# Clamped cross attention: the limits moved from the scores to the probabilities

## The chip, the cores and the metric

One core of a Trainium2 chip runs the whole program in one launch. The metric is the device time of that launch in microseconds; lower is better.

## The reference

A perceiver with 32 sequences of 32 tokens of 256 channels and a context of 257 rows of 192 channels for each sequence. Fourteen stages follow one another, among them four cross attentions. Two of these, of level 0 and level 1, are computed by the function that is changed. What they compute:

```
q = layernorm(x) @ Wq + bq        # 16 heads of 16
k = ctx @ Wk + bk;  v = ctx @ Wv + bv
s = scale * q @ k.T
s = clip(s, -10000, 10000)        # level 1 only
p = softmax(s)                    # over 257 context rows
x = x + (p @ v) @ Wo + bo
```

## The kernel before

`cross_attention` (L738) handles one sequence after another; the text calls one a batch, n = 0 to 31, and four of them a group (128 tokens). The engines' programs are written out by hand as queues that meet in semaphores. The order of each queue is fixed, and an instruction that waits holds all behind it.

For batch n, TensorE (`keys_values`) makes the keys and values of batch n + 1 from the context, turns the probabilities of batch n (`turn_probs`, L833: two pairs of score rows, four transposes each, each pair behind its own `probs_ready`) and then makes the scores of batch n + 1 (`scores`, L816). In the second and third batch of a group two of four parts of the products with values of the previous group stand between these (`probs_values`, L847, L853), in the fourth the turning of its outputs and the output product.

ScalarE (`exponentials`, L937) computes exp(score + nmax) for four rows of 257 columns in two pairs; between the pairs it evicts the keys of the next batch (`take_keys`, L927). Behind them comes its copy of the turned probabilities (L957).

VectorE (`maxima`, L1065) reduces each pair of score rows to the negated maximum `nmax`. With a clamp, L1062 first writes the clamped scores to the tile `sc` in SBUF, and both the reduction and the exponential read `sc`; without one both read PSUM. Its queue in a batch is: normalise the outputs (fourth batch of a group only, L1075 and L1077), evict the values (L1053), add to x (first batch only, L1082), round the context of batch n + 3 (L1048), copy the turned probabilities (L1108), mask the tails (first batch, L1069), statistics (third batch, L1086), maxima of n + 1.

GpSimd splits the context behind VectorE's rounding (L987, L990), spreads the queries (L979) and keeps the 257th column of the probabilities (L996) once both pairs are ready. SyncE loads the context three batches ahead.

The level 0 stage runs from about 22 to 213 us of the span, the level 1 stage, with `clamp=1.0e4`, from about 568 to 773 us. Only the latter has L1062.

Of the kernel before, what the change touches and what calls it, by code (L numbers as in the profile page):

```python
# [18 lines left out]
ALU = mybir.AluOpType  # L19
ACT = mybir.ActivationFunctionType  # L20
# [3 lines left out]
P = 128  # L24
# [713 lines left out]
def cross_attention(k, w, qt, given, clamp=None):  # L738

    nc = k.nc  # L740
# [4 lines left out]
             "tails_ready values_placed turned_done turned_act turned_dve tails_turned tail_masked pv_done rsum_ready o_ready ot_done "  # L745
             "ot_ready y_done y_added noted")
    with stage(k, names) as (block, s), \
            buffers(k, t0=[P, B], t1=[DK - P, B], vtail=[B, 16, 17], key=[P, 2, DC, LK], val=[P, 2 * BT, 2, 16, 17], qx=[P, 2, DC, 2, S],
                    p=[P, 2, 4, LK], nmax=[P, 2, 4], pt=[P, 2 * BT, 2, 4, DC, 2, S], tails=[P, 2, P], tail_values=[P, 2, 16, 17],
                    own_tails=[P, BT, DC, 2, S], rsum=[P, 16], o=[P, 16, 16], ot=[P, DC, P],  # L750
                    sc=[P, 4 if clamp else 1, LK if clamp else 1]) as b, \
            buffers(k, F32R, w=[P, 2, 2, 2 * D], c=[P, 3, 2, LP], clo=[P, 3, LP]) as r:
# [170 lines left out]
        def _(act):  # L923
# [6 lines left out]
            def exponentials(n, par, first):  # L930
                if not first:
                    act.wait_ge(s.tails_ready, n - 1)
                for r4 in range(4):
                    if r4 % 2 == 0:
                        act.wait_ge(s.max_ready, 2 * n + 1 + r4 // 2)
                    score = b.sc[:, r4, :] if clamp else k.ps[:, SB + r4, 0:LK]
                    last = nc.scalar.activation(b.p[:, par, r4, :], score, ACT.Exp, bias=b.nmax[:, par, r4:r4 + 1])  # L937
                    if r4 % 2:
                        last.then_inc(s.probs_ready, 1)
                    if r4 == 1 and n + 1 < B:  # L940
                        take_keys(n + 1, 1 - par)
# [19 lines left out]

            act.wait_ge(*w.at)
            for u, part in ((0, w.wk), (1, w.wv)):
                nc.scalar.copy(r.w[:, 0, :, u * D:(u + 1) * D], part).then_inc(s.w_hi, 1)
# [10 lines left out]
        def _(pool):  # L975
# [26 lines left out]
            def body(it, first, last):  # L1002
                for gpar in range(2):
                    group = 2 * it + gpar
                    for j in range(BT):
# [12 lines left out]
                        if not (last and gpar == 1 and j == BT - 1):  # L1018
                            keep_tails(n + 1, (j + 1) % 2, gpar if j < BT - 1 else 1 - gpar, (j + 1) % BT)

            for t, ordered in ((given.t0, b.t0), (given.t1, b.t1)):
                nc.gpsimd.tensor_copy(ordered[:].rearrange("p (b t) -> p b t", b=BT),
                                      t[:].rearrange("p (t b) -> p b t", b=BT)).then_inc(s.t_ordered, 1)
                pool.wait_ge(s.t_ordered, 1 if ordered is b.t0 else 2)
# [18 lines left out]
        def _(dve):  # L1043
# [12 lines left out]
            def maxima(n, par):  # L1056
                dve.wait_ge(s.scores_done, n + 1)
                for half in range(2):
                    rs = slice(2 * half, 2 * half + 2)
                    score = k.ps[:, SB + rs.start:SB + rs.stop, 0:LK]  # L1060
                    if clamp:
                        nc.vector.tensor_scalar(b.sc[:, rs, :], score, clamp, -clamp, ALU.min, ALU.max).then_inc(s.clamped, 1)  # L1062
                        dve.wait_ge(s.clamped, 2 * n + 1 + half)
                        score = b.sc[:, rs, :]
                    nc.vector.tensor_reduce(b.nmax[:, par, rs], score, AX.X, ALU.max, negate=True).then_inc(s.max_ready, 1)  # L1065

# [25 lines left out]
            def body(it, first, last):  # L1092
                for gpar in range(2):
                    group = 2 * it + gpar
                    begin, end = first and gpar == 0, last and gpar == 1
                    for j in range(BT):
                        n = group * BT + j
                        final = end and j == BT - 1
                        if j == 3 and not begin:
                            normalize_outputs(group - 1)  # L1100
                        if not final:
                            take_values(n + 1, gpar * BT + j + 1 if j < BT - 1 else (1 - gpar) * BT)
# [2056 lines left out]
```

## Time and profile before

| | |
|---|---|
| median of 3 runs | 1841.16 us (1838.53 to 1845.12) |
| the profiled execution | 1834.88 us |
| its span, first to last instruction | 1833.0 us |
| PE matmul busy | 1553.4 us (85%) |
| DVE busy | 964.6 us (53%) |
| ACT busy | 748.2 us (41%) |
| POOL busy | 534.4 us (29%) |
| mean granted clock of TensorE | 0.928 of full speed |

Shares of the whole span are averages over fourteen stages with different limits, so this table does not say what an edit to one stage is worth. PE is TensorE's matmul, DVE is VectorE, ACT is ScalarE, POOL is GpSimd. Durations of matmuls overlap, since they are pipelined, and neighbouring instructions of an engine overlap at their ends too; the distance between two starts is then shorter than the duration of the first.

### The profile page before, as it was taken

Reading aid. Unit: us, or ns where it says so; the run is one execution under the profiler, and the core shown is the slowest. Engines: PE = TensorE matmul, PEld = TensorE weight load, DVE = VectorE, ACT = ScalarE, POOL = GpSimd, SP = SyncE. Lnnn points to the kernel's source line nnn. Section 1 sums busy time; section 2 is a strip of 40 time slices with the busy share of each in tenths; the row PEclk is TensorE's granted clock in tenths of the full one; section 3 lists DMA queues with packets and bytes.
Section 4 is the critical chain, followed back from the end, with each engine's and each line's share of the span. In section 5 each row is a group of like instructions: output and inputs, shape, how many; then the busy total and the mean of one; then the engine's idle time right before and its main releaser. Section 6 shows DMA issues by size and latency. Waiting matters only on the chain. (4 is left out here: it accounts for less than half of the span.)

```text
span 1833.0 us, 44725 instructions
## 1 busy us (share of the span) xinstructions
PE 1553.4 (85%) x17451; PEld 1311.3 (72%) x17451; DVE 964.6 (53%) x2131; ACT 748.2 (41%) x1714; POOL 534.4 (29%) x699
## 2 busy tenths in 40 slices
PE   6999745799996999795999879997787998888894
PEld 5888644599975777674888768984675985666784
DVE  5666468611117888657222257664655773466323
ACT  3555455333433555351233236663133423445122
POOL 3444235032213443160444222220011210433341
PEclk9999877899998999897999989999887999898897
DMA  4211010198862111021899743330101119311696
GB/s 146 53 51 44 6 41 11 58 352 321 330 225 80 49 49 49 7 50 72 283 319 313 265 150 102 91 92 11 45 2 39 46 52 289 84 33 43 208 314 206
DMA packets 103107, 228.36 MB, mean 125 GB/s; under 512 B 36184, under 2 KB 56152, under 8 KB 95776
## 3 DMA queue, kind: packets, MB, share of 16 engines
q1 hardware_dynamic: 91008, 200.06, 33.8%
q0 software_dynamic: 8160, 22.29, 3.2%
q10 hardware_dynamic: 3776, 3.67, 0.6%
q8 instruction: 122, 2.00, 0.4%
q14 instruction: 41, 0.34, 0.1%
HBM read 206.12 MB, written 19.79 MB: 123 GB/s over the span
## 5 line engine op out<-in xcount | busy, mean ns | idle before, releaser
L2434 PEld LDWEIGHTS ps<-xt,w 128*128 128x128 f32 x1728 | 202.3, 192 | 37.8 <-issue 26.2
L2434 PE MATMUL ps<-xt,w 128*128 128x128 f32 x1728 | 211.2, 278 | 18.4 <-DMA w<-in_L_ffn_w 14.4
L2487 ACT ACTIVATE g<-ps,b 128x128 f32<-128x128 f32 x340 | 124.3, 367 | 245.1 <-PE ps L2434 220.5
L2444 PE MATMUL ps<-w,g 128*128 128x256 f32 x864 | 200.7, 379 | 0.3 <-ACT g L2487 0.3
L2444 PEld LDWEIGHTS ps<-w,g 128*128 128x128 f32 x864 | 157.5, 190 | 18.5 <-ACT g L2487 0.6
L2528 POOL DMA_INDIRECT results<-y,dest x85 | 83.8, 986 | 253.8 <-DVE y L2656 253.8
L2648 DVE COPY xt<-ps 128x256 f32<-128x256 f32 x85 | 36.1, 424 | 195.4 <-PE ps L2424 195.4
L2523 POOL DMA_INDIRECT x<-rows,token x85 | 82.7, 973 | 166.8 <-DVEq L2623 141.8
L2656 DVE COPY y<-ps 128x256 f32<-128x256 f32 x85 | 36.1, 425 | 161.9 <-PE ps L2444 161.9
L797 PE MATMUL ps<-c,w 128*128 128x258 f32 x512 | 93.4, 294 | 7.7 <-DVE pt L1108 6.4
L937 ACT ACTIVATE p<-sc,nmax 128x257 f32<-128x257 f32 x128 | 58.1, 503 | 81.3 <-DVE nmax L1065 81.3
L441 PE MATMUL ps<-consts_sb,z_sb 128*128 128x128 f32 x176 | 39.6, 416 | 59.2 <-DVE z_sb L627 59.2
L807 PE MATMUL ps<-w,c 128*128 128x256 f32 x512 | 89.2, 287 | 0.1
L797 PEld LDWEIGHTS ps<-c,w 128*128 128x128 f32 x512 | 74.7, 189 | 19.9 <-issue 17.7
L1053 DVE TENSOR_TENSOR val<-ps,store_sb 128x512 f32<-128x512 f32 x64 | 44.2, 690 | 82.3 <-PE ps L807 82.1
L2129 PE MATMUL ps<-x,w 128*128 128x512 f32 x288 | 78.8, 414 | 7.7 <-DVE w L2292 7.7
L459 PE MATMUL ps<-x,w 128*128 128x512 f32 x336 | 81.1, 399 | 3.5 <-DVE x L639 2.4
L604 POOL TENSOR_TENSOR w<-store_sb,w 128x512 fp32r<-128x512 f32 (+1 forms) x20 | 26.7, 1351 | 196.4 <-DVE z_sb L627 148.5
L441 PEld LDWEIGHTS ps<-consts_sb,z_sb 128*128 128x128 f32 x176 | 34.3, 218 | 64.3 <-DVE z_sb L627 63.2
L833 PE MATMUL ps<-consts_sb,p 128*128 128x128 f32 x512 | 75.0, 281 | 5.1 <-ACT key L927 2.2
L2142 PEld LDWEIGHTS ps<-w,g 128*128 128x128 f32 x576 | 74.9, 191 | 4.2 <-DVE g L2245 0.5
L459 PEld LDWEIGHTS ps<-x,w 128*128 128x128 f32 x336 | 64.1, 194 | 19.1 <-DVE x L639 6.2
(452 smaller groups left out, 3554.2 us busy)
## 6 DMA issues: line engine op xcount, KB each, us to landing
w<-in_L_ffn_w SPq DMA_DIRECT2D x124, 512.0 KB, 5.0
w<-in_L_ffn_w SPq DMA_DIRECT2D x46, 1024.0 KB, 5.1
c<-in_ctx SPq DMA_DIRECT2D x96, 258.0 KB, 2.7
rows<-in_w_L_xattn SPq DMA_DIRECT2D x32, 192.0 KB, 2.6
rows<-in_w_L_xattn SPq DMA_DIRECT2D x8, 768.0 KB
values<-v SPq DMA_DIRECT2D x8, 544.0 KB, 3.1
vx<-values SPq DMA_DIRECT2D x32, 136.0 KB, 3.4
c<-in_w_L_xattn SPq DMA_DIRECT2D x8, 514.0 KB
```

The source lines that it names most:

```text
L441: mm = nc.tensor.transpose(k.ps[:, 2 * half + c, t * P:(t + 1) * P], z[:, half * HT + t, c * P:(c + 1) * P], k.ident)
L459: mm = nc.tensor.matmul(bank, r.w[:, p1, c, col:col + P], r.x[:, p2, c, half * 512:(half + 1) * 512], start=i == 0 and c == 0, stop=i == 2 ...
L797: last = nc.tensor.matmul(k.ps[:, KB + c, 0:LP], wp, cp, start=t == 0, stop=t == 4)
L807: last = nc.tensor.matmul(k.ps[:, VB, half * D:(half + 1) * D], cp, wp, start=t == 0, stop=t == 4)
L833: last = nc.tensor.transpose(k.ps[:, TB + pair, at:at + P], b.p[:, par, r4, half * P:(half + 1) * P], k.ident)
L2129: mm = nc.tensor.matmul(k.ps[:, slot(j, h), :], r.w1[:, j // 2, p1, c, h * P:(h + 1) * P], r.x[:, p2, c, (j % 2) * 512:(j % 2 + 1) * 512], ...
L2142: mm = nc.tensor.matmul(k.ps[:, 4 + t, 0:D], r.g[:, p1, slot(j, h), t * P:(t + 1) * P], r.w2[:, j // 2, p2, h, :], start=h == 0 and i == 0 ...
L2434: mm = nc.tensor.matmul(hidden_bank(par, h), b.w1[:, par, c, h * P:(h + 1) * P], b.xt[:, par, c, :], start=c == 0, stop=c == DC - 1)
L2444: mm = nc.tensor.matmul(k.ps[:, YB + par, 0:D], b.g[:, par, h, :], b.w2[:, par, h, :], start=h == 0, stop=h == HC - 1)
L2487: nc.scalar.activation(b.g[:, par, h, :], hidden_bank(par, h), func, bias=b.b1[:, par, h:h + 1]).then_inc(s.g_ready, 1)
L2523: nc.gpsimd.indirect_dma_start(b.x[:, n % 4, :], None, k.rows, bass.IndirectOffsetOnAxis(ap=u.token[:, n:n + 1], axis=0)).then_inc(x_loade ...
L2528: nc.gpsimd.indirect_dma_start(k.results, bass.IndirectOffsetOnAxis(ap=u.dest[:, n:n + 1], axis=0), b.y[:, n % 2, :], None).then_inc(sent[ ...
```

## The change

With a clamp, the scores are no longer clamped. The reduction reads PSUM, a small VectorE instruction clamps the two negated maxima, and the exponential reads PSUM. Behind each pair ScalarE computes `low` = exp(nmax - clamp), the probability that a score at the lower limit has, with the bias tile `floor`. VectorE then raises each probability to at least `low` and lowers it to at most 1 in place (`bound`), and only that releases `probs_ready`. The two calls of `bound` stand ahead of the eviction of the values in VectorE's queue, with the normalisation between them. The tile `sc` goes, `floor` and `low` come, with two semaphores. The memset of `floor` on GpSimd and ScalarE's wait for it are in both stages.

```diff
--- before.py
+++ after.py
@@ -743,12 +743,12 @@
     names = ("t_ordered ctx_loaded0 ctx_loaded1 ctx_loaded2 w_hi w_split ctx_hi ctx_low ctx_split tail_done ones_set tail_ready tail_placed cleared "
              "x_ready keys_done values_done keys_ready values_ready spread_ready scores_done clamped max_ready probs_ready "
              "tails_ready values_placed turned_done turned_act turned_dve tails_turned tail_masked pv_done rsum_ready o_ready ot_done "
-             "ot_ready y_done y_added noted")
+             "ot_ready y_done y_added noted raised floor_set")
     with stage(k, names) as (block, s), \
             buffers(k, t0=[P, B], t1=[DK - P, B], vtail=[B, 16, 17], key=[P, 2, DC, LK], val=[P, 2 * BT, 2, 16, 17], qx=[P, 2, DC, 2, S],
                     p=[P, 2, 4, LK], nmax=[P, 2, 4], pt=[P, 2 * BT, 2, 4, DC, 2, S], tails=[P, 2, P], tail_values=[P, 2, 16, 17],
                     own_tails=[P, BT, DC, 2, S], rsum=[P, 16], o=[P, 16, 16], ot=[P, DC, P],
-                    sc=[P, 4 if clamp else 1, LK if clamp else 1]) as b, \
+                    floor=[P, 1], low=[P, 2, 4]) as b, \
             buffers(k, F32R, w=[P, 2, 2, 2 * D], c=[P, 3, 2, LP], clo=[P, 3, LP]) as r:
         ctx_loaded = [s.ctx_loaded0, s.ctx_loaded1, s.ctx_loaded2]
         low = slice(DK - P, P)
@@ -933,10 +933,12 @@
                 for r4 in range(4):
                     if r4 % 2 == 0:
                         act.wait_ge(s.max_ready, 2 * n + 1 + r4 // 2)
-                    score = b.sc[:, r4, :] if clamp else k.ps[:, SB + r4, 0:LK]
-                    last = nc.scalar.activation(b.p[:, par, r4, :], score, ACT.Exp, bias=b.nmax[:, par, r4:r4 + 1])
+                    last = nc.scalar.activation(b.p[:, par, r4, :], k.ps[:, SB + r4, 0:LK], ACT.Exp, bias=b.nmax[:, par, r4:r4 + 1])
                     if r4 % 2:
-                        last.then_inc(s.probs_ready, 1)
+                        if clamp:
+                            last = nc.scalar.activation(b.low[:, par, r4 - 1:r4 + 1], b.nmax[:, par, r4 - 1:r4 + 1], ACT.Exp,
+                                                        bias=b.floor[:, 0:1])
+                        last.then_inc(s.raised if clamp else s.probs_ready, 1)
                     if r4 == 1 and n + 1 < B:
                         take_keys(n + 1, 1 - par)
 
@@ -960,6 +962,7 @@
                             exponentials(n + 1, (j + 1) % 2, begin and j == 0)
 
             act.wait_ge(*w.at)
+            act.wait_ge(s.floor_set, 1)
             for u, part in ((0, w.wk), (1, w.wv)):
                 nc.scalar.copy(r.w[:, 0, :, u * D:(u + 1) * D], part).then_inc(s.w_hi, 1)
             take_keys(0, 0)
@@ -1018,6 +1021,7 @@
                         if not (last and gpar == 1 and j == BT - 1):
                             keep_tails(n + 1, (j + 1) % 2, gpar if j < BT - 1 else 1 - gpar, (j + 1) % BT)
 
+            nc.gpsimd.memset(b.floor[:], -clamp if clamp else 0.0).then_inc(s.floor_set, 1)
             for t, ordered in ((given.t0, b.t0), (given.t1, b.t1)):
                 nc.gpsimd.tensor_copy(ordered[:].rearrange("p (b t) -> p b t", b=BT),
                                       t[:].rearrange("p (t b) -> p b t", b=BT)).then_inc(s.t_ordered, 1)
@@ -1058,11 +1062,19 @@
                 for half in range(2):
                     rs = slice(2 * half, 2 * half + 2)
                     score = k.ps[:, SB + rs.start:SB + rs.stop, 0:LK]
+                    top = nc.vector.tensor_reduce(b.nmax[:, par, rs], score, AX.X, ALU.max, negate=True)
                     if clamp:
-                        nc.vector.tensor_scalar(b.sc[:, rs, :], score, clamp, -clamp, ALU.min, ALU.max).then_inc(s.clamped, 1)
+                        top.then_inc(s.clamped, 1)
                         dve.wait_ge(s.clamped, 2 * n + 1 + half)
-                        score = b.sc[:, rs, :]
-                    nc.vector.tensor_reduce(b.nmax[:, par, rs], score, AX.X, ALU.max, negate=True).then_inc(s.max_ready, 1)
+                        top = nc.vector.tensor_scalar(b.nmax[:, par, rs], b.nmax[:, par, rs], clamp, -clamp, ALU.min, ALU.max)
+                    top.then_inc(s.max_ready, 1)
+
+            def bound(n, par, half):
+                dve.wait_ge(s.raised, 2 * n + half + 1)
+                for r4 in range(2 * half, 2 * half + 2):
+                    last = nc.vector.tensor_scalar(b.p[:, par, r4, :], b.p[:, par, r4, :], b.low[:, par, r4:r4 + 1], 1.0,
+                                                   ALU.max, ALU.min)
+                last.then_inc(s.probs_ready, 1)
 
             def mask_tails(group):
                 dve.wait_ge(s.tails_turned, group + 1)
@@ -1096,8 +1108,12 @@
                     for j in range(BT):
                         n = group * BT + j
                         final = end and j == BT - 1
+                        if clamp:
+                            bound(n, j % 2, 0)
                         if j == 3 and not begin:
                             normalize_outputs(group - 1)
+                        if clamp:
+                            bound(n, j % 2, 1)
                         if not final:
                             take_values(n + 1, gpar * BT + j + 1 if j < BT - 1 else (1 - gpar) * BT)
                         if j == 0 and not begin and not (first and gpar == 1):
```

## Rows read from the trace of the kernel before

**Rows 1.** Windows: stretch, its length, busy us (instructions) by engine, granted clock, DMA.

```profile
628.69:651.76 23.07, 22.15 (x473) 18.39 (x473) 19.04 (x34) 12.31 (x29) 9.51 (x22) 1.00 0.18 49
...
99.73:121.50 21.77, 21.45 (x473) 18.38 (x473) 13.36 (x26) 12.14 (x29) 9.21 (x22) 1.00 0.20 52
```

**Rows 2.** Groups by line, 578 to 760 us.

```profile
L937 ACT ACTIVATE p<-sc,nmax 128x257 f32<-128x257 f32 x128 | 58.1, 503 | 81.3 <-DVE nmax L1065 81.3
...
L1062 DVE TENSOR_SCALAR sc<-ps 128x514 f32<-128x514 f32 x64 | 43.8, 685 | 0.3 <-PE ps L816 0.3
```

**Rows 3.** Groups by line, 32 to 201 us.

```profile
L937 ACT ACTIVATE p<-ps,nmax 128x257 f32<-128x257 f32 x128 | 53.8, 478 | 54.5 <-DVE nmax L1065 54.5
```

**Rows 4.** Waits, 578 to 760 us: total, times, longest.

```profile
ACT p L937 <- DVE nmax L1065: 81.3, 33, 4.1
...
DVE pt L1108 <- PE ps L833: 9.2, 18, 0.9
```

**Rows 5.** Timeline of DVE, 628 to 652 us: start, duration, instruction.

```profile
638.39 0.69 DVE L1053 TENSOR_TENSOR val<-ps,store_sb 128x512 f32<-128x512 f32 x1 [1.59 <-PE ps L807]
639.00 0.42 DVE L1048 CAST c<-c 128x516 fp32r<-128x516 f32 x1
639.33 0.68 DVE L1108 COPY pt<-ps 128x512 f32<-128x512 f32 x1
639.93 0.42 DVE L1086 BATCH_NORM_STATS2 stats_sb<-x_sb 128x6 f32<-128x256 f32 x1
640.26 0.68 DVE L1062 TENSOR_SCALAR sc<-ps 128x514 f32<-128x514 f32 x1
640.98 0.69 DVE L1065 TENSOR_REDUCE nmax<-sc 128x2 f32<-128x514 f32 x1
...
645.10 0.69 DVE L1108 COPY pt<-ps 128x512 f32<-128x512 f32 x1 [0.56 <-PE ps L833]
645.79 0.69 DVE L1062 TENSOR_SCALAR sc<-ps 128x514 f32<-128x514 f32 x1
...
650.57 0.68 DVE L1108 COPY pt<-ps 128x512 f32<-128x512 f32 x1
651.17 0.68 DVE L1069 TENSOR_TENSOR own_tails<-ps,consts_sb 128x512 f32<-128x512 f32 x1
651.76 0.68 DVE L1062 TENSOR_SCALAR sc<-ps 128x514 f32<-128x514 f32 x1
```

**Rows 6.** Timeline of ACT, 628 to 652 us.

```profile
641.76 0.91 ACT L937 ACTIVATE p<-sc,nmax 128x257 f32<-128x257 f32 x2 [2.35 <-DVE nmax L1065]
642.58 0.82 ACT L927 ACTIVATE key<-ps,store_sb 128x257 f32<-128x257 f32 x2
643.29 0.90 ACT L937 ACTIVATE p<-sc,nmax 128x257 f32<-128x257 f32 x2
```

**Rows 7.** Timeline of PE, 628 to 652 us.

```profile
643.98 1.09 PE L833 MATMUL ps<-consts_sb,p 128*128 128x128 f32 x8
645.00 0.69 PE L816 MATMUL ps<-key,qx 32*64 32x257 f32 x16
```

**Rows 8.** Timeline of ACT, 1250 to 1258 us.

```profile
1254.55 0.30 ACT L527 ACTIVATE std<-mv_sb,consts_sb 128x8 f32<-128x8 f32 x1 [4.72 <-PEq L228]
1254.76 0.28 ACT L529 ACTIVATE std<-mv_sb,consts_sb 128x8 f32<-128x8 f32 x1
```

**Rows 9.** Instructions of three lines: duration ns, least/median/most.

```profile
L1696 DVE TENSOR_SCALAR far<-sn,consts_sb x32: 343/486/590, 293.2 to 323.7; 128x256 f32<-128x256 f32 x32
L1696 DVE TENSOR_SCALAR kx<-kt,consts_sb x12: 337/350/354, 799.0 to 1648.7; 128x256 f32<-128x256 f32 x12
...
L2588 DVE TENSOR_SCALAR count<-count x3: 172/173/174, 356.3 to 1698.2; 128x8 f32<-128x8 f32 x2, 128x16 f32<-128x16 f32 x1
...
L2936 DVE TENSOR_SCALAR pb<-consts_sb,p x8: 229/230/231, 1519.8 to 1557.9; 128x4 f32<-128x4 f32 x8
```

**Rows 10.** Groups by line of ACT, whole span.

```profile
L1299 ACT ACTIVATION_READ_ACCUMULATOR p<-ps,nmax 128x1 f32 x64 | 12.9, 201 | 0.0
```

## The prediction

> **What bounds the kernel now.** The change touches one function, and only its use with a clamp computes differently, so I read the stages before the whole. The windows of busy time [rows 1] show two uses of the same cross attention with the same matmuls. Four batches of the first use, without a clamp, took 21.77 us and PE was busy 21.45 us of them (99%); four batches of the clamped one took 23.07 us with PE busy 22.15 us (96%) and DVE busy 19.04 us instead of 13.36 us. So the clamp costs some 1.3 us a group of four batches, 8 groups, 10 us in all. That is the most that this edit could give back.
>
> Next the groups by line [rows 2, 3]: the clamp is 64 DVE instructions of 685 ns, and the exponentials are 503 ns from SBUF against 478 ns from PSUM. The waits [rows 4] say that ScalarE idles 81.3 us of the 182 for the maxima, while DVE waits only 9.2 us for transposed probabilities: ScalarE is not short of capacity, it stands in a serial loop. The timeline shows the loop: scores, clamp, maximum, exponential (DVE to ScalarE), transposes on PE, DVE's copy of them, the next maxima. In the batch that begins at 640.26 [rows 5 to 7], the maximum of the first half ends at 641.67, the exponentials begin 0.09 us later, the last of them ends at 644.19 (3.93 us after the loop began), the transposes end at 645.07, the copy starts at 645.10, and the next clamp at 645.79: 5.53 us. PE's own queue has 21.45 to 22.15 us of work for four batches, so the loop may take 5.4 us on average before it sets the pace. Whatever puts the last probability later than some 3.9 us after the loop's start, or stretches DVE's own work behind it, is paid nearly in full.
>
> **What the change removes.** Per batch two clamps on DVE. Each is followed by a dependent reduction 0.72 us later (640.26 to 640.98, [rows 5]), so 1.44 us of DVE's time and, on the way to the first exponential, 0.72 us. Exponentials read PSUM again: start to start about 0.365 us instead of 0.41, by the durations of a pair (0.91 less 0.503, [rows 2, 6]; 0.478 less the overlap of 0.11 for PSUM, [rows 3]). The first use of the function is left as it was except for a one-column memset on POOL that ScalarE now waits for at the stage's start; POOL's first work is on the way to the first scores, so it counts: between nothing and the 0.20 us of the smallest instruction [rows 10] each, I take 0.3 us for the two together.
>
> **What it adds on DVE.** (a) Two bounds of the 128x2 maxima. The nearest row is a tensor_scalar with two constants, 173 ns [rows 9]. It waits for the reduction as the reduction waited for the clamp (0.04 us behind its end), so about 0.21 us on the way to each exponential. Lower bound 0.17 us, the wait hidden; upper 0.27 us, if it takes 0.23 as the 128x4 one with an operand per partition [rows 9]. (b) Four passes over 128x257 of probabilities with one per-partition operand and one constant. The nearest rows are a tensor_scalar with one per-partition operand on 128x256 in SBUF: 350 ns where nothing else reads SBUF much, and 486 ns median in a stage where its neighbours are busy [rows 9]. The lower bound is the shortest of these, 0.337 us, the upper one that median, 0.486. I take 0.35 us, and 0.275 us start to start (DVE's neighbours in the timeline overlap by 0.07 to 0.09 us: 638.39 to 639.00 for an instruction of 0.69 [rows 5]), because POOL's splitting of context runs after DVE's cast, at the end of the loop, not in the middle where the bounds fall. The Trainium skill, page "VectorE: DVE Perf Modes", section "The perf-mode tier table", lets a single-source fp32 operation between SBUF tiles run at two elements per cycle, and "What auto-detection actually checks" grants that to an odd length too if source and destination agree. No row before has an odd length, so the trace neither confirms nor denies it for 257; by it the bound is the 0.35 us that I take, without it near the upper bound.
>
> DVE's own work thus falls by 1.44 us and grows by 2 x 0.21 + 4 x 0.275 = 1.52 us per batch. There is no relief of DVE, only a change of where its work stands.
>
> **What it adds on ScalarE.** Two exponentials on 128x2 with a bias per partition, one behind each pair. The nearest rows are two activations with such a bias on 128x8: 0.30 us, start to start 0.21 [rows 8]. The first probabilities are released only behind it, and the second pair 0.21 us later. The lower bound is the smallest instruction that ScalarE ran behind an exponential, 0.20 us [rows 10], 0.10 of it on the queue with the overlap of neighbours; the upper one 0.30. Taken: 0.30 and 0.22.
>
> **The new loop**, from the start of the first reduction (time 0). First maximum 0.68, bounded 0.89, exponential starts 0.98 (0.09 as at 641.67 to 641.76), small exponential 0.98 + 2 x 0.365 = 1.71, ends 2.01; key evictions start 1.93, second pair 2.65 (0.72 later, as 642.58 to 643.29, [rows 6]), small one 3.38 to 3.68. The second maximum is bounded at 1.75 and is not late. DVE's first bounds run from 2.10 to about 2.7. The second ones start 3.77 and end 4.39. So the last probability is ready 4.39 us after the loop's start instead of 3.93: the 0.51 us gained at the head (0.98 for 1.50 us) are more than spent.
>
> Then what is queued behind the waiting bounds. DVE waits at the second pair from about 2.7 to 3.77 for ScalarE, and the eviction of the values, the addition to x, the cast of the context and the copy of transposed probabilities all stand behind it, where before they filled this wait. From 4.32: values 0.61, cast 0.33 ([rows 5], 638.39, 639.00, 639.33), copy from 5.26 to the next maxima 0.60, so they start at 5.87. PE's transposes of the second pair begin at 4.43, its scores end at 5.64: PE is not the last. DVE now sets the loop at 5.87 us, before extras. In one batch of four there are the addition (0.33) and the mask (0.60, 651.17 to 651.76), in one the statistics (0.33, 639.93 to 640.26); the normalisation falls into the idle time between the two bounds. A group is 4 x 5.87 + 1.26 = 24.7 us; with PE's own queue followed through the two batches that hold the products with values, whose transposes come later, about 25.0 us. I take 24.95, against 23.07 measured: 1.88 us a group, 8 groups 15.0 us, 0.6 us for the bounds of the last batch and 0.3 for the memsets: +16 us. PE's share of the group falls to 22.15 / 24.95 = 89%, in idle pieces under 1 us; the granted clock is 1.00 in all the windows [rows 1] and I leave it there.
>
> The profiled execution took 1834.88 us (span 1833.0), 6.3 us under the median of 1841.16. The sum makes 1851 of it; added to the median, **1857 us**.
>
> The same page of the Trainium skill, section on the TRN2 errata, says that operations with a source in SBUF pay a fixed extra per instruction and advises tiles of 512 elements or more. That speaks against this change: two instructions of 514 columns from PSUM become six, of 2 and 257 columns, from SBUF. The trace agrees in kind: the 2-to-8-column instruction costs 173 ns for next to no elements. It alters nothing in the sum, which has the durations of rows.
>
> **Rivals.** (1) *The bounds run at one element per cycle or are held up by POOL*: 0.486 us each, 0.41 start to start. Each pair ends 0.27 us later and so does all behind: the loop is about 6.15 us, the group 26.05, and the time +24 + 0.9, about 1866. For it: the 486 ns median; against: 350 ns in 12 quieter ones. (2) *No change within 0.3%* (5.5 us, about what a measurement of this kernel can tell from no change). The loop may then grow by 0.17 us on average, to 5.94 from 5.77 (23.07 / 4), where I have 6.24. With the small exponential at 0.20 (0.10 on the queue) and the bounds at 0.337 the loop is 5.61 and the group 24.2 us, which is still +9 us. No change needs something more: that waits of PE and DVE, which I add up in order, overlap, or that the values' eviction finds its way out from behind the bounds' wait at no cost. Time 1841 to 1846, I take 1844. (3) *Faster*: the clamp's 0.72 us at the head is all that counts, DVE's queue behind the bounds is hidden since values and cast need not be early, and PE is again the bound, as in the first use. Then a group is 21.8 us, 8 x 1.27 = 10 us less, 1831. It decides at the last probability: ready by 3.4 to 3.9 us it would hold. The trace speaks against: even with the cheapest of the unknown costs it is 4.15. (4) *The clamp's removal does nothing*, since DVE had slack: it idled 4.0 us in the group of 23.07 [rows 1], but the windows of the two uses show that the loop with the clamp is longer; in size that is rival 2.
>
> **Chances.** Likeliest (bounds at about 0.35 us, +7 to +21 us): 0.57. Rival 1: 0.22. Rivals 2 and 4: 0.13. Rival 3: 0.08. So slower by over 0.3% 0.79, within 0.13, faster 0.08. The range leaves out the faster case and most of no change: from 1845 (+4, under the +9 of all lower ends by what the adding up may be off) to 1869 (+28, rival 1's +25 and the bounds of the maxima at 0.23 us with something over).
>
> **What would show it.** In the changed profile, by step: the 128x2 tensor_scalar near 173 ns; the 128x2 exponential near 300; the pass over 128x257 near 350, not 486; exponentials at 478; the time from first reduction to end of second bound 4.4 us; DVE idle before the second bounds for ScalarE about 1 us in each batch and hardly before the copy; the interval between first maxima of following batches about 5.9, with 6.8 and 6.3 where the extras are; the stage some 15 us longer; everything outside this stage equal within 1 us. I am wrong if the bounds fall into DVE's former waits without moving the copy, if ScalarE overlaps its small exponentials wholly, or if the pass is much dearer.

## The result and the profile after

The changed kernel takes 1857.43 us (median of 5, 1854.33 to 1863.71) where the kernel before takes 1842.94 (median of 5): the ratio is 1.0086, 95% interval 1.0056 to 1.0116. It is slower, by 14.5 us between the medians and by some 16 us by the ratio (10 to 21 by its interval).

The page of its profiled execution:

```profile
span 1854.9 us, 44921 instructions
...
PE 1558.4 (84%) x17451; PEld 1316.4 (71%) x17451; DVE 969.4 (52%) x2259; ACT 755.6 (41%) x1778; POOL 532.6 (29%) x701
```

VectorE's busy time grew from 964.6 to 969.4 us and ScalarE's from 748.2 to 755.6, far less than the span; what grew is waiting. To see where, I measure the stage itself from the start of the addition that makes the tails' values (VectorE, once at the stage's head) to the start of the last normalisation. That stretch of the level 1 stage was 576.2 to 770.3 us, 194.1 us, and is now 575.9 to 785.8, 209.9 us: +15.8 us, as much as the whole 0.86%. The same stretch of the level 0 stage was 178.9 us and is 179.5. The two profiled spans differ by 22 us; the other 6 lie behind the level 1 stage, where the change touches nothing. What stands there is the same in every kernel of this text and took 1062.7 us in the profile before, the least of all fourteen, and 1064.2 to 1073.2 in the others, so this difference is scatter between executions.

A stage is read from one profiled execution each. Where the level 0 stage has the same instruction order (all kernels but the one with the keys last) its stretch came out between 178.6 and 181.2 us. Differences of a stage below some 2 us are therefore not told from none.

One group of four batches, in the windows of busy time:

```profile
652.63:677.57 24.94, 22.40 (x472) 18.40 (x472) 19.57 (x51) 13.42 (x37) 9.24 (x22) 1.00 0.17 45
```

24.94 us, at a granted clock of 1.00, with PE at 90%. It is the group that begins with the thirteenth batch of the stage, which took 22.98 us before; the 23.07 of [rows 1] is the one that begins with the tenth, and those four batches take 25.09 us now. So a group grew by 1.96 to 2.02 us. The added instructions by line (duration in ns, least, median, most):

```profile
L939 ACT ACTIVATE low<-nmax,floor x64: 291/301/327, 578.8 to 774.5; 128x2 f32<-128x2 f32 x64
...
L1075 DVE TENSOR_SCALAR p<-p,low x128: 345/350/358, 581.1 to 775.3; 128x257 f32<-128x257 f32 x128
...
L1069 DVE TENSOR_SCALAR nmax<-nmax x64: 168/170/426, 577.9 to 773.4; 128x2 f32<-128x2 f32 x64
```

The timeline of VectorE over the first batch of that group, which answers to [rows 5]:

```profile
652.63 0.68 DVE L1065 TENSOR_REDUCE nmax<-ps 128x2 f32<-128x514 f32 x1
653.34 0.41 DVE L1069 TENSOR_SCALAR nmax<-nmax 128x2 f32<-128x2 f32 x1
653.67 0.68 DVE L1065 TENSOR_REDUCE nmax<-ps 128x2 f32<-128x514 f32 x1
654.38 0.17 DVE L1069 TENSOR_SCALAR nmax<-nmax 128x2 f32<-128x2 f32 x1
654.90 0.62 DVE L1075 TENSOR_SCALAR p<-p,low 128x257 f32<-128x257 f32 x2 [0.35 <-ACT low L939]
656.58 0.62 DVE L1075 TENSOR_SCALAR p<-p,low 128x257 f32<-128x257 f32 x2 [1.06 <-ACT low L939]
657.11 0.69 DVE L1057 TENSOR_TENSOR val<-ps,store_sb 128x512 f32<-128x512 f32 x1
657.71 0.41 DVE L1094 TENSOR_TENSOR x_sb<-x_sb,ps 128x256 f32<-128x256 f32 x1
658.04 0.42 DVE L1052 CAST c<-c 128x516 fp32r<-128x516 f32 x1
658.38 0.69 DVE L1124 COPY pt<-ps 128x512 f32<-128x512 f32 x1
658.98 0.68 DVE L1081 TENSOR_TENSOR own_tails<-ps,consts_sb 128x512 f32<-128x512 f32 x1
659.58 0.68 DVE L1065 TENSOR_REDUCE nmax<-ps 128x2 f32<-128x514 f32 x1
```

and of ScalarE, which answers to [rows 6]:

```profile
653.85 0.84 ACT L936 ACTIVATE p<-ps,nmax 128x257 f32<-128x257 f32 x2 [2.06 <-DVE nmax L1069]
654.58 0.29 ACT L939 ACTIVATE low<-nmax,floor 128x2 f32<-128x2 f32 x1
654.79 0.84 ACT L927 ACTIVATE key<-ps,store_sb 128x257 f32<-128x257 f32 x2
655.53 0.84 ACT L936 ACTIVATE p<-ps,nmax 128x257 f32<-128x257 f32 x2
656.24 0.31 ACT L939 ACTIVATE low<-nmax,floor 128x2 f32<-128x2 f32 x1
```

The loop is in these two. The reduction starts at 652.63, the exponentials at 653.85, the small one for the second pair ends at 656.55, and VectorE, which has done nothing since its first bounds ended at 655.5, starts the second bounds at 656.58. They end at 657.20, 4.57 us after the loop's start, where in the kernel before the last probability was ready after 3.93. Only then come the values, the addition, the cast, the copy, the mask, one behind another without a gap, and the next reduction at 659.58. The waits of the stage, total, times and longest, say the same and answer to [rows 4]:

```profile
ACT p L936 <- DVE nmax L1069: 84.2, 32, 3.7
DVE p L1075 <- ACT low L939: 40.4, 61, 1.9
...
DVE pt L1124 <- PE ps L833: 2.3, 3, 2.0
```

VectorE's wait for PE's transposes has gone from 9.2 us (11.6 with the last batches, to 770 us) to 2.3, nearly all of it one wait in the last batch, since elsewhere VectorE is late for them now; a new wait of 40.4 us for ScalarE stands in the middle of its queue.

### The profile page after: what moved, and what is told of

Read it like the earlier page. It is cut to its first block and busy times, and to the rows that moved or that the text cites. A ratio compares the mean times of both kernels' runs of the same rounds, so it can differ in the third digit from the quotient of the medians.

```text
span 1854.9 us, 44921 instructions
## 1 busy us (share of the span) xinstructions
PE 1558.4 (84%) x17451; PEld 1316.4 (71%) x17451; DVE 969.4 (52%) x2259; ACT 755.6 (41%) x1778; POOL 532.6 (29%) x701
## 3 DMA queue, kind: packets, MB, share of 16 engines
q8 instruction: 121, 1.98, 0.4%
## 5 line engine op out<-in xcount | busy, mean ns | idle before, releaser
L2460 PE MATMUL ps<-w,g 128*128 128x256 f32 x864 | 200.8, 380 | 0.0
L936 ACT ACTIVATE p<-ps,nmax 128x257 f32<-128x257 f32 x256 | 107.9, 479 | 138.9 <-DVE nmax L1069 84.2
L1065 DVE TENSOR_REDUCE nmax<-ps 128x2 f32<-128x514 f32 x128 | 84.8, 683 | 0.5 <-PE ps L816 0.5
L2158 PE MATMUL ps<-w,g 128*128 128x256 f32 x576 | 76.4, 283 | 0.8 <-issue 0.3
```

Source lines behind the costliest of these rows:

```text
L936: last = nc.scalar.activation(b.p[:, par, r4, :], k.ps[:, SB + r4, 0:LK], ACT.Exp, bias=b.nmax[:, par, r4:r4 + 1])
L1065: top = nc.vector.tensor_reduce(b.nmax[:, par, rs], score, AX.X, ALU.max, negate=True)
L2158: mm = nc.tensor.matmul(k.ps[:, 4 + t, 0:D], r.g[:, p1, slot(j, h), t * P:(t + 1) * P], r.w2[:, j // 2, p2, h, :], start=h == 0 and i == 0 ...
L2460: mm = nc.tensor.matmul(k.ps[:, YB + par, 0:D], b.g[:, par, h, :], b.w2[:, par, h, :], start=h == 0, stop=h == HC - 1)
```

## The experiments

Each kernel was timed against the kernel before on the same chip. "Stage" is the stretch defined above; it is 194.1 us in the kernel before and 209.9 in the changed one. A group is four batches in mid-stage, from the first reduction (or clamp) of the thirteenth batch to that of the seventeenth. The stages are single profiled executions, the ratios are of 4 to 10 runs with 17 to 25 of the kernel before, the changed kernel's of 5 with 5. The intervals of the ratios reach 3 to 8 us to either side, and several of the steps below overlap by them; the readings rest on the stages.

| kernel | ratio to before (interval) | stage us | group us |
|---|---|---|---|
| before | | 194.1 | 22.98 |
| changed | 1.0086 (1.0056 to 1.0116) | 209.9 | 24.94 |
| no small exponentials | 1.0050 (1.0026 to 1.0074) | 201.9 | 23.90 |
| first bounds doubled | 1.0110 (1.0075 to 1.0146) | 211.5 | 24.98 |
| second bounds doubled | 1.0193 (1.0148 to 1.0238) | 225.8 | 27.05 |
| keys evicted last | 1.0049 (1.0029 to 1.0069) | 197.8 | 23.36 |
| no bounds of probabilities | 0.9959 (0.9942 to 0.9976) | 185.9 | 22.37 |
| no bounds of maxima | 1.0069 (1.0045 to 1.0094) | 203.8 | 24.47 |
| cast ahead of second bounds | 1.0071 (1.0045 to 1.0098) | 207.0 | 24.33 |
| maxima bounded with two tensors | 1.0088 (1.0060 to 1.0116) | 209.1 | 24.99 |
| no clamp at all | 0.9918 (0.9888 to 0.9949) | 178.8 | 21.72 |
| limit column | 1.0040 (1.0021 to 1.0060) | 200.3 | 23.88 |
| limit column, keys last | 0.9962 (0.9945 to 0.9980) | 190.3 | 22.49 |
| the same, cast ahead | 0.9965 (0.9951 to 0.9980) | 189.5 | 22.53 |

**Does the place of the work count, or its amount?** The theory: one serial loop sets the pace, and work is paid where it stands on that loop. The rivals: VectorE's total work, or ScalarE's. Two kernels add the same VectorE work, 64 passes of 0.275 us start to start, 17.6 us in all, once before the wait and once behind it (the diff is the first; the second has `half == 1`).

```diff
             def bound(n, par, half):
                 dve.wait_ge(s.raised, 2 * n + half + 1)
                 for r4 in range(2 * half, 2 * half + 2):
+                    if half == 0:
+                        nc.vector.tensor_scalar(b.spare[:, r4 % 2, :], b.p[:, par, r4, :], b.low[:, par, r4:r4 + 1], 1.0,
+                                                ALU.max, ALU.min)
```

> The changed kernel with each bound of the first pair made twice (the extra pass writes a spare row). VectorE gets 2 x 0.275 us more per batch, at a place where it has idled about 1 us before the second bounds. Loop theory: hidden but for the batch with the normalisation between the bounds, +0 to +3 us, 1857 to 1860. Rival 'VectorE's work': 32 x 0.55 = +17.6 us, 1875, as much as for the second pair.

> The changed kernel with each bound of the second pair made twice. The same added work as in the run with the first pair doubled, but behind the wait. Loop theory: paid in full, 32 x 0.55 = +17.3 us, 1875; a group takes 27.1 us. Rival 'VectorE has slack' (idle 5.4 us of a group of 24.94): +0 to +3 us. If both doublings cost the same, the place does not matter and the loop theory is wrong.

Measured: +1.6 us of stage for the first pair, +15.9 us for the second. VectorE of the first kernel, where the four passes fill the wait:

```profile
643.59 0.36 DVE L1076 TENSOR_SCALAR spare<-p,low 128x257 f32<-128x257 f32 x1 [0.65 <-ACT low L939]
...
644.39 0.35 DVE L1078 TENSOR_SCALAR p<-p,low 128x257 f32<-128x257 f32 x1
645.24 0.62 DVE L1078 TENSOR_SCALAR p<-p,low 128x257 f32<-128x257 f32 x2 [0.50 <-ACT low L939]
645.89 0.69 DVE L1057 TENSOR_TENSOR val<-ps,store_sb 128x512 f32<-128x512 f32 x1
```

The four passes run from 643.59 to 644.74, the wait before the second bounds is 0.50 us instead of 1.0, and they start 4.23 us after the loop's start, as in the changed kernel (640.25 to 644.49, 4.24 us, in the batch of the same place). In the other kernel nothing is left behind the wait to take them up, and the values start 1.06 us after the second bounds instead of 0.53:

```profile
635.68 0.62 DVE L1078 TENSOR_SCALAR p<-p,low 128x257 f32<-128x257 f32 x2 [0.36 <-ACT low L939]
637.38 0.36 DVE L1076 TENSOR_SCALAR spare<-p,low 128x257 f32<-128x257 f32 x1 [1.08 <-ACT low L939]
...
638.44 0.68 DVE L1057 TENSOR_TENSOR val<-ps,store_sb 128x512 f32<-128x512 f32 x1
```

The amount is the same and the price is next to nothing in one place (+1.6 us is within the scatter of a stage) and nearly the whole in the other. The ratios say the same more coarsely: 0.24 points more than the changed kernel for the first pair, 1.07 for the second. VectorE's total work is refuted as the cause, and so is the reading that VectorE has slack because it idles 5.4 us in a group.

**What is ScalarE's share?**

```diff
-                        if clamp:
-                            last = nc.scalar.activation(b.low[:, par, r4 - 1:r4 + 1], b.nmax[:, par, r4 - 1:r4 + 1], ACT.Exp,
-                                                        bias=b.floor[:, 0:1])
...
+            nc.gpsimd.memset(b.low[:], 0.0)
```

> The changed kernel without the two small exponentials of a batch; the lower bounds are a constant 0 that is written once. It leaves out the computation of exp(nmax - clamp). Loop theory (the last probability and VectorE's queue behind the second bounds set the pace): both pairs are released 0.18 and 0.40 us earlier, a group of four batches takes 23.8 us in place of 24.94, the stage is 9 us shorter, 1848 us. Rival 'ScalarE': the small exponentials are the whole loss of the change, so the time returns to that of the kernel before, 1842. Rival 'VectorE's work': what counts is the sum of VectorE's instructions, which stays, so 1857.

Stage 8.0 us shorter than the changed one, group 23.90 us (the lower bounds are a constant 0 here, written once by GpSimd). About half of the loss is the small exponentials, half remains: the rival that they are the whole of it fell.

**The bounds of the probabilities.** Here both calls of `bound` are left out, and the small exponential releases the probabilities.

```diff
             def bound(n, par, half):
-                dve.wait_ge(s.raised, 2 * n + half + 1)
-                for r4 in range(2 * half, 2 * half + 2):
-                    last = nc.vector.tensor_scalar(b.p[:, par, r4, :], b.p[:, par, r4, :], b.low[:, par, r4:r4 + 1], 1.0,
-                                                   ALU.max, ALU.min)
-                last.then_inc(s.probs_ready, 1)
+                return
```

> The changed kernel without the four passes over the probabilities; the small exponentials stay and release them. It leaves out the bounding of the probabilities. Loop theory: no wait of VectorE for ScalarE in mid-queue, the values and the cast fill that time again, the last probability is ready 0.7 us earlier; a group takes 22.1 us, 24 us less than the changed kernel, 1834, and under the kernel before. Rival 'ScalarE' (the small exponentials are most of the loss): at most half of that, 1845 or more.

Stage 24.0 us shorter, group 22.37 us, and the kernel is faster than before (0.9959). The 128 passes are 35 us start to start; by the doublings the first pair's are nearly free and the second pair's paid, some 16 to 18 us. With them goes the wait in mid-queue, behind which the values and the cast stood; that the rest of the 24 us is this wait is a reading and was not measured by itself. The window of one group and the longest wait of VectorE in the stage:

```profile
646.21:668.58 22.37, 21.85 (x472) 18.37 (x473) 15.08 (x34) 13.31 (x37) 9.43 (x22) 1.00 0.20 51
```

```profile
DVE val L1057 <- PE ps L807: 48.9, 31, 3.1
```

VectorE now waits 48.9 us for PE's values, and PE is at 98% of the group: it is the bound again.

**The bounds of the maxima.**

```diff
-                    if clamp:
-                        top.then_inc(s.clamped, 1)
-                        dve.wait_ge(s.clamped, 2 * n + 1 + half)
-                        top = nc.vector.tensor_scalar(b.nmax[:, par, rs], b.nmax[:, par, rs], clamp, -clamp, ALU.min, ALU.max)
                     top.then_inc(s.max_ready, 1)
```

> The changed kernel without the two bounds of the negated maxima. It leaves out the clamping of the maxima. Loop theory: 0.21 us less ahead of the first exponential, and 0.25 more of it in the batches in which the instruction took 0.42 us; a group takes 24.3 to 24.6 us, the stage is 4 to 8 us shorter, 1850 to 1853. Rival: hidden, since VectorE waits for ScalarE afterwards anyway: 1857.

Stage 6.1 us shorter. The forecast was 4 to 8. These 64 instructions of two columns are on the loop, at its head.

**What stands in VectorE's queue behind the second bounds.**

```diff
                         if j == 3 and not begin:
                             normalize_outputs(group - 1)
+                        if clamp and n + 3 < B:
+                            round_context(n + 3)
                         if clamp:
                             bound(n, j % 2, 1)
```

> The changed kernel with the cast of the context moved ahead of the second bounds, into VectorE's wait. Loop theory: 0.33 us per batch leaves the queue behind the bounds, of which TensorE's transposes, next in line, let through 0.24 in the batches without products with values; 4 us less, 1853; a group takes 24.4 us. Rival 'only VectorE's queue counts': 0.33 x 32 = 10.6 us less, 1847. Rival 'only the last probability counts': no change.

Stage 2.9 us shorter, group 24.33: near the 4 us of the loop theory, far from the 10.6 of the rival; no change, the other rival, is not far outside the scatter of a stage, but every group of mid-stage is shorter, by 0.1 to 0.6 us. Once the queue is 0.33 us shorter, PE's transposes are next in line and take most of it back; the copy waits for them (0.15 to 0.18 us) where it did not before.

**ScalarE's order.**

```diff
-                    if r4 == 1 and n + 1 < B:
+                    if r4 == 3 and n + 1 < B:
                         take_keys(n + 1, 1 - par)
```

> The changed kernel with ScalarE's eviction of the next keys moved from between the two pairs of exponentials to behind the second. Nothing is left out. Loop theory: the second pair is released 0.72 us earlier (2.96 us after the loop's start), the keys are there at 3.75 us, just when TensorE needs them to turn; a group takes 23.3 us and the stage is 12 us shorter, 1846. Rival: the keys come late instead, TensorE turns nothing before they are evicted, and the time stays at 1857. Rivals 'VectorE's work' and 'ScalarE's work': no work is taken away, so 1857.

```profile
652.84 0.85 ACT L936 ACTIVATE p<-ps,nmax 128x257 f32<-128x257 f32 x2 [1.53 <-DVE nmax L1069]
653.58 0.29 ACT L939 ACTIVATE low<-nmax,floor 128x2 f32<-128x2 f32 x1
653.77 0.84 ACT L936 ACTIVATE p<-ps,nmax 128x257 f32<-128x257 f32 x2
654.48 0.30 ACT L939 ACTIVATE low<-nmax,floor 128x2 f32<-128x2 f32 x1
654.67 0.84 ACT L927 ACTIVATE key<-ps,store_sb 128x257 f32<-128x257 f32 x2
```

The stage is 12.1 us shorter without an instruction less on any engine: the second pair begins 0.93 us after the first instead of 1.68, and the keys go last. Both rivals that count work say 0. The whole kernel gained less than the stage (0.37 points of ratio, some 7 us), and part of the reason is in the other stage: the edit holds there too, and its stretch grew from 179.5 to 182.5 us, beyond what it varies by without the edit. There the late keys hold up the start of PE's transposes; this wait of the level 0 stage (total, times, longest) is not in the changed kernel:

```profile
PEld ps L833 <- ACT key L927: 3.1, 8, 0.6
```

**The small instruction beside GpSimd.**

```diff
-                        top = nc.vector.tensor_scalar(b.nmax[:, par, rs], b.nmax[:, par, rs], clamp, -clamp, ALU.min, ALU.max)
+                        top = nc.vector.scalar_tensor_tensor(b.nmax[:, par, rs], b.nmax[:, par, rs], clamp, b.lows[:],
+                                                             ALU.min, ALU.max)
```

> The changed kernel with the bound of the maxima as an instruction of two tensors (minimum with the constant, maximum with a 128x2 tile of the lower limit), the same function. In the trace of the changed kernel this small instruction ends with GpSimd's pass over the context where they meet, 0.42 us instead of 0.17. Theory of the shared way to SBUF: with two tensors as input it runs at its 0.17 to 0.23 us beside GpSimd, and 16 batches gain up to 0.25 us, 0 to 4 us less, 1853 to 1857. Rival: GpSimd's instruction delays any of VectorE's that reads SBUF, so it stays 0.42.

No gain (209.1 us, ratio 1.0088), and the instruction is held in the same way, in 17 of the 32 batches as in the changed kernel; the rival was right in this. GpSimd and VectorE of this kernel:

```profile
656.51 0.73 POOL L993 TENSOR_TENSOR c<-c 64x258 fp32r<-64x258 f32 x1
```

```profile
656.13 0.68 DVE L1068 TENSOR_REDUCE nmax<-ps 128x2 f32<-128x514 f32 x1
656.85 0.41 DVE L1072 SCALAR_TENSOR_TENSOR nmax<-nmax,lows 128x2 f32<-128x2 f32 x1
```

**How much there was to gain.**

```diff
-                    cross_attention(k, w, b.qt, b, clamp=1.0e4 if name == "L1_xattn" else None)
+                    cross_attention(k, w, b.qt, b, clamp=None)
```

> The kernel before with no clamp in the level 1 stage, so that both stages run the same program. It leaves out the clamp altogether, and it is the most that any edit of the clamp can give while the rest stays. By the windows of the two stages before: a group takes 21.8 us in place of 23.07, the stage is 10 to 12 us shorter, about 1832 where the kernel before has 1843. If the clamp was hidden before, nothing changes.

15.3 us of stage, 0.9918. It is more than expected. The first group has no products with values between its batches, PE has less to do, and there more of the clamp was paid: from the first batch's reduction or clamp to the fifth's it took 22.60 us before (577.50 to 600.10) and takes 19.08 now (577.37 to 596.45), 3.5 us where a group in mid-stage gives 1.3. The last group and what follows it give 4.2 (from its start to the last normalisation 31.57 us, now 27.34). The windows of mid-stage show neither.

**A version that is faster than both.** The small exponentials can go without leaving anything out. A 258th column of the score banks holds -clamp, the exponential runs over it, and its result is the lower bound of the row. (Not shown in the cuts: the columns that keep TensorE busy at the stage's start move to another bank, TensorE waits for the memset, and the memset on GpSimd goes.)

```diff
-                    last = nc.scalar.activation(b.p[:, par, r4, :], k.ps[:, SB + r4, 0:LK], ACT.Exp, bias=b.nmax[:, par, r4:r4 + 1])
+                    last = nc.scalar.activation(b.p[:, par, r4, :], k.ps[:, SB + r4, 0:LP], ACT.Exp, bias=b.nmax[:, par, r4:r4 + 1])
...
-                        if clamp:
-                            last = nc.scalar.activation(b.low[:, par, r4 - 1:r4 + 1], b.nmax[:, par, r4 - 1:r4 + 1], ACT.Exp,
-                                                        bias=b.floor[:, 0:1])
...
-                    last = nc.vector.tensor_scalar(b.p[:, par, r4, :], b.p[:, par, r4, :], b.low[:, par, r4:r4 + 1], 1.0,
-                                                   ALU.max, ALU.min)
+                    row = b.p[:, par, r4, 0:LK]
+                    last = nc.vector.tensor_scalar(row, row, b.p[:, par, r4, LK:LP], 1.0, ALU.max, ALU.min)
...
+            nc.vector.memset(k.ps[:, SB:SB + 4, LK:LP], -clamp if clamp else 0.0).then_inc(s.floor_set, 1)
```

> The changed kernel, the same function, with the small exponentials gone: a 258th column of each score bank in PSUM holds -clamp for good (one memset at the stage's start), the exponential runs over 258 columns, and the probability of that column is the lower bound that the passes over the row read. Loop theory: as in the run without the small exponentials, 8 us less than the changed kernel in the stage (201.9 from start to last normalisation where the changed one has 209.9), 1850. Rival: the 258th column or the new wait costs as much, 1857.

Stage 200.3 us, 9.6 less than the changed one, and a group of 23.88 us as without the small exponentials (23.90). So their cost was avoidable as far as these runs can tell. It is still slower than before (1.0040), and the next run puts the keys last as well, in the clamped stage alone:

```diff
-                    if r4 == 1 and n + 1 < B:
+                    if r4 == (3 if clamp else 1) and n + 1 < B:
```

> The same with the eviction of the next keys behind both pairs of exponentials, in the clamped stage alone (in the run that moved it in both stages, the stage without a clamp grew by 3.0 us). Same function. Loop theory: a group takes 22.5 us, the stage 191.7 us where the kernel before has 194.1, so 2 us less than before, 1840 to 1841. Rival: once ScalarE's wait is gone TensorE's own order with late keys costs more than the 3 us of the other stage, and it stays above before, 1846.

Stage 190.3 us, group 22.49: 0.9962 of the kernel before, interval 0.9945 to 0.9980, and computing the same as the changed kernel. VectorE in one batch of it, and its wait for ScalarE in the stage (total, times, longest):

```profile
647.05 0.69 DVE L1062 TENSOR_REDUCE nmax<-ps 128x2 f32<-128x514 f32 x1
...
649.03 1.35 DVE L1073 TENSOR_SCALAR p<-p 128x257 f32<-128x257 f32 x4 [0.17 <-ACT p L937]
650.45 0.69 DVE L1054 TENSOR_TENSOR val<-ps,store_sb 128x512 f32<-128x512 f32 x1
```

```profile
DVE p L1073 <- ACT p L937: 5.4, 31, 0.2
```

All four bounds run as one block 1.98 us after the loop's start and the wait in mid-queue is 5.4 us in the stage instead of 40.4.

One more step is the cast ahead of the second bounds, as above:

> The same with the cast of the context ahead of the second bounds as well. Theory: VectorE's queue is not what the loop waits for any more, so the cast's own 0.33 us gives nothing; GpSimd, which follows the cast, finishes earlier and the small bounds of the maxima no longer meet it (0.25 us in up to half of the batches), 0 to 3 us less than the run before, 1837 to 1841. Rival: the cast now stands ahead of bounds that are ready earlier and delays them, 2 to 5 us more.

Stage 189.5 us, 0.9965: no difference from the run before that the intervals show.

## Why the prediction was right

It named 1857 us and the time is 1857.43. The mechanism is as forecast; that the two agree to half a microsecond is luck. The median of the kernel before moved from 1841.16 to 1842.94 us with two more runs, so the measured difference is 14.5 us by medians and some 16 by the ratio, where +16 was forecast. By its steps:

- **The loop.** Right, and shown by the doubled bounds and by the moved keys. A group was to take 24.95 us and takes 24.94 in the window above, 24.5 to 25.9 over the groups of the stage; the stage grew by 15.8 us for a predicted 15.6, and the starts of the stages by 0.4 for 0.3. The last probability was to be ready after 4.39 us and is after 4.57 where the small instruction is held up, 4.33 where it is not (659.58 to 663.91).
- **Durations.** The pass over 257 columns takes 350 ns, as taken; the small exponential 301 ns; the small VectorE instruction about 170 to 200 ns in 47 cases of 64. The rule of the Trainium skill, page "VectorE: DVE Perf Modes", section "What auto-detection actually checks", that an odd length too gets two elements per cycle if source and destination agree, had no row before; with 350 ns for 257 columns as for 256 [rows 9], the trace now agrees. With it rival 1 (0.486 us) fell. Its price could have been settled from the trace before: those of the 32 instructions of [rows 9] that ran beside a GpSimd pass took up to 0.59 us, and the six that met none took 0.343 to 0.347. None of the 128 passes over the probabilities meets a GpSimd instruction. The forecast reads "2-to-8-column instruction" from a row of 8 and 16 columns; the new rows have two columns, at 170 ns. The same kind of instruction with 16 columns from PSUM took 171 ns (L1712), so these rows show a fixed price for a small instruction, but none that is SBUF's own.
- **The queue behind the second bounds.** Right: from 656.58 to the next reduction the timeline has 0.53, 0.60, 0.33, 0.34, 0.60, 0.60 us; the sum had 0.55, 0.61, 0.33, 0.33, 0.60, 0.60. In the batch after it the same stretch without extras takes 2.07 us (663.29 to 665.36), predicted 2.10.
- **Single intervals** between first reductions: 6.95, 5.78, 6.46 and 5.75 us, predicted 6.8, 5.87, 6.2 to 6.3 and 5.87. The first and third are longer and the others shorter than said, so part of the agreement of the sum is luck: the forecast's own terms make 24.74 us, and it put 0.2 on top for PE's queue in two batches, without rows for it. Of this the intervals show 0.1 us, in the third, where the keys come late. What was missed and stood in its place is at the head: the small instruction takes 0.41 to 0.42 us instead of 0.17 in two batches of four, in 17 of the stage's 32. It was taken as fixed at 173 ns. In the third of these intervals its price was smaller, since ScalarE waits for PE's keys anyway (they come at 667.63, 1.04 us after the first exponentials' start, where 0.92 is usual).
- **The ceiling.** "10 us in all, the most that this edit could give back" was too small: 15.3 us. It was taken from mid-stage windows; the first and the last group were not looked at. The forecast did not rest on it, but rival 3 (faster, 1831) did, and it could have been worth 5 us more.
- **The start of the stages.** 0.3 us for the two memsets. From VectorE's first cast to the addition at the head of the stretch, level 0 took 8.40 us (22.15 to 30.55) and takes 8.53 (23.20 to 31.73), level 1 took 8.58 and takes 8.83: 0.4 us together. In the three kernels with the limit column, where this memset is gone and the wait stands later, the two are 8.38 to 8.40 and 8.56 to 8.58 again. No run separates the memset from the wait.
- **A slip in rival 2.** Its cheapest case has a loop of 5.61 us and calls the group 24.2. Four loops and the extras of 1.26 make 23.7, with the 0.2 for PE 23.9, so the cheapest case was +7 to +8 us and not +9. It is still clear of no change, and the chances did not turn on it.
- **A sign that did not come.** "Everything outside this stage equal within 1 us" was too strict: outside it the two profiled executions differ by 6 us where nothing was changed.
- **Rivals 2 to 4** fell: what makes the kernel faster, the freed head of the loop, is real (the kernel without the bounds is below before), but the bounds take more than that.

## What to carry to other kernels

Before moving work to "an engine with slack", find the loop through the engines and write down when the last result of each turn is ready; an instruction costs its full time if it is on that loop or queued behind a wait on it, and next to nothing if it falls into the wait (1.6 against 15.9 us here). A new wait costs what is queued behind it on its engine, and this can be more than the work itself: look at whether the engine that is waited for can do it earlier (the keys last) or need not do it at all (the limit as one more column). An order that pays in one stage can cost in the next one that shares the code: 12 us less in one, 3 us more in the other here.

## What the runs showed of the hardware

A VectorE instruction of two columns in SBUF, 170 ns by itself, was held to the end of a GpSimd pass that ran at the time. In the changed kernel this befell 17 of 64, each the first of its batch, and all 17 ended 0.03 us behind the end of the pass. GpSimd in the changed kernel:

```profile
652.19 0.73 POOL L990 TENSOR_TENSOR clo<-c 128x258 fp32r<-128x258 f32 x1 [0.73 <-DVE c L1052]
653.00 0.73 POOL L993 TENSOR_TENSOR c<-c 64x258 fp32r<-64x258 f32 x1
```

GpSimd's pass ends at 653.73; VectorE's small instruction of 653.34 ends at 653.75, after 0.41 us. The reduction that reads PSUM beside the same passes takes its usual 0.68. So does the mask, which reads PSUM and one tile in SBUF (658.98, beside GpSimd's next pass), and a statistics instruction that reads one SBUF tile took its usual 0.42 us beside a pass of GpSimd, here and in four other batches:

```profile
671.05 0.73 POOL L990 TENSOR_TENSOR clo<-c 128x258 fp32r<-128x258 f32 x1 [0.73 <-DVE c L1052]
```

```profile
671.49 0.42 DVE L1098 BATCH_NORM_STATS2 stats_sb<-x_sb 128x6 f32<-128x256 f32 x1
```

Reading SBUF at the time is therefore not enough to be held. The small instruction with two tensors as input was held likewise (656.85, 0.41 us, ending at 657.26, GpSimd at 657.24), so of the two forms tried for it neither passes. The Trainium skill, page "VectorE: DVE Perf Modes", section "Two Vector instructions with no wait between them", speaks of a second read interface to SBUF that VectorE shares with GpSimd and uses both for a second tensor and in the two-port modes; both forms of the small instruction are of these kinds. The section gives no time for it; the trace agrees in that these two were held, and the reduction and the mask, with at most one tensor in SBUF and one in PSUM, were not, nor the statistics, with one tensor and at 0.42 us for 256 columns slower than the 0.35 us of [rows 9]. That the second interface is the reason was not shown by itself.
